# A three-layer graph attention pipeline: score rows of the heads by DMA through DRAM, first values and x one slot earlier

## The chip, the core and the metric

The kernel runs on one core of a Trainium2 chip. The metric is the device time of one execution in microseconds. Its engines are TensorE (PE in the profile), VectorE (DVE), ScalarE (ACT), GpSimd (POOL) and SyncE (SP), which issues all DMAs here. Each works through its own instructions in order; semaphores tie them together. PEld is TensorE's loading of weights.

## The reference, cut to what is computed

There are 16 graphs (batches) of 512 nodes, 256 features and a random adjacency. Layer 1 is attention with four heads of 128 features and an ELU, layer 2 attention with one head of 256, both with the diagonal added to the mask. Then comes a residual with x and a layer norm; layer 3 is one more attention (mask without the diagonal), a leaky ReLU, a residual and a layer norm.

```
def gat_layer(x, mask, W, a_src, a_dst, bias, concat):
    xl = (x @ W).reshape(B, N, H, F)
    asrc = einsum('bnhf,hf->bnh', xl, a_src)
    adst = einsum('bnhf,hf->bnh', xl, a_dst)
    e = leaky_relu(asrc[:, :, None, :] + adst[:, None, :, :], 0.2)
    e = where(mask[..., None], e, -1e9)
    out = einsum('bsdh,bshf->bdhf', softmax(e, axis=1), xl)
...
h = elu(gat_layer(x, mask, W1, ..., concat=True))
h = gat_layer(h, mask, W2, ..., concat=False)
x = layernorm(x + h)
...
Wh = x @ W
e = where(adj > 0, leaky(s_i[:, :, None] + s_j[:, None, :]), -9e15)
x = layernorm(x + leaky(einsum('bij,bjf->bif', softmax(e, axis=1), Wh)))
```

## The kernel before

One attention of one batch is a unit: a head (h0 to h3) of layer 1, the L2 of layer 2, the L3 of layer 3. Units are laid into slots, six to a batch. Slot 0 of batch n has L3 of batch n-3, slots 1 to 4 have the heads of batch n, slot 5 has L2 of batch n-1. Every engine's program is a loop over slots (g, with `n, pos = divmod(g, 6)`), and in it the order of the steps is written out by hand.

A unit takes these steps. `sources_row` (TensorE, line 476 through `spread`) lays the sources' scores as a row over all partitions, with four transposes into the PSUM bank bA, two slots ahead. `tops` (VectorE, line 949, in the slot ahead) adds that row to the turned mask mask_t and takes the largest, four instructions for the four blocks of nodes; `shifted_targets` (lines 962 and 967) makes low and b_t of it, four columns each. `targets_row` (TensorE, line 476 with bB) spreads b_t as a row. In the unit's own slot ScalarE makes leaky (line 741) and exp (756 for heads, 753 for L2, 760 for L3), and VectorE masks with mask_n (`keep_edges`, lines 1000 and 996). In the slot behind, TensorE attends in two halves (`attend`, lines 516, 527, 538). For a head, VectorE then inverts the sums (980), ScalarE normalizes (768) and makes exp (776), VectorE finishes the ELU (974), TensorE turns it (506), and ScalarE and VectorE split it into a high and a low part (782, 986).

Beside the units the slots carry the dense products. First values: `turn_x` (579) turns x, `x_out` (787) and `x_low` (1010) split it, `values_1` (625, 628) multiplies block by block, `values_1_out` (809) copies to val1, which has two buffers. For batch n+1 x is turned in slot 0 of batch n, and the blocks are made in slots 1, 2, 5 and 5. Second values (610) are in slots 2 and 3, third values (598) in slot 4, the turning of x1 (589) in slot 3.

GpSimd has, in order: `scale_3` (419) in slot 0; the scale of the first norm (385, 388), `residual_2` (433, after the first norm x1n of the same slot) and `set_diag` (425) in slot 2; `add_bias_2` (411, after b_t of h3) in slot 3; `norm_2` (385, 388, 394) in slot 4. VectorE's statistics for it (`norm_stats`, 1039 and 1042) stand in slot 5, and `make_mask` (1005) in slot 0. SP issues per batch: four turnings of the mask, the loads of adj and x, the store of an output.

Of the kernel before, what the change touches and what calls it, by code (L numbers as in the profile page):

```python
# [32 lines left out]


def gat_kernel(nc, x, adj, W1, as1, ad1, b1, W2, as2, ad2, b2, W3, a3, out):
# [15 lines left out]
    FIRST, LAST = -SLOTS, SLOTS * B  # L51
# [15 lines left out]

    for i, u in enumerate(units.values()):
        u.u = i
    for i, u in enumerate(u for u in units.values() if u.row):  # L70
        u.r = i

# [11 lines left out]
    with ExitStack() as ctx:  # L84
# [53 lines left out]
        x1_t = sb("x1_t", [P, KD, N])  # L138
        act3 = sb("act3", [P, NB, D])
# [52 lines left out]
        out_stored = sem("out_stored")  # L192

# [59 lines left out]
        for g in range(FIRST, LAST + 1):  # L253
# [19 lines left out]
        for m in (END - 2, END - 1, END):  # L273
            parts = range(len(PARTS) if m == END else 2)
            thirds[m].use = [len(u_uses) + i for i in parts]
            u_uses += [(act3_ready, m * 2 + i + 1) for i in parts]

# [26 lines left out]
        def _(sp):  # L304
# [14 lines left out]

            def turn_mask(n):  # L320
# [26 lines left out]
            load_x(1)  # L347
            for n in range(-1, B):
# [4 lines left out]
                if 2 <= n + 2 < B:  # L353
                    load_x(n + 2)
                if n >= 3:
                    store(n - 3, range(NB))
# [7 lines left out]
        def _(pool):  # L364
# [70 lines left out]
            for g in range(FIRST, LAST):  # L435
# [29 lines left out]
        def _(pe):  # L465
# [13 lines left out]
            def sources_row(u):  # L479
# [6 lines left out]
                if u.u:  # L486
                    pe.wait_ge(top_done, u.u * NB)
# [157 lines left out]
            def first_heads(g):  # L645
# [14 lines left out]
                if g == 5:  # L660
                    sources_row(units[SLOTS + 1])
                if before:
                    attend(before, 1)
                if g == 3:
                    weight_sums()

            pe.wait_ge(consts, 9)
            spread_weights()
            for g in range(FIRST, LAST + 1):
# [9 lines left out]
                if pos == 0 and batch:  # L679
                    turn_x(n + 1)  # L680
                if pos == 2 and batch:
                    values_1(n + 1, 1)
# [4 lines left out]
                if pos == 5 and batch:  # L687
                    values_1(n + 1, 2)
# [6 lines left out]
                if pos == 1 and batch:  # L695
                    if n == -1:
                        pe.wait_ge(w1_lo_ready, 1)
                        pe.wait_ge(bias1_ready, 2 * G)
                    values_1(n + 1, 0)
# [8 lines left out]
                if pos == 5 and batch:  # L708
                    values_1(n + 1, 3)
                if before:  # L710
                    attend(before, 1)
                if later and g < LAST:
                    sources_row(later)
            turn_head(final_head)
# [19 lines left out]
        def _(act):  # L734
# [84 lines left out]
            def first_heads(g):  # L819
# [19 lines left out]
                if g == 5:  # L839
                    act.wait_ge(folded, 2 * KD * H + G + 2 * KH)  # L840
# [4 lines left out]
            for g in range(FIRST, LAST + 1):  # L845
# [6 lines left out]
                if g == -SLOTS:  # L852
                    for k in range(KD):
                        act.wait_ge(w1_in[k], 16 * G)
                        nc.scalar.copy(w1_hi[:, k, :, 0:HC], w1[:, k, :, 0:HC]).then_inc(w1_hi_ready, 1)
# [7 lines left out]
                if pos == 5 and batch:  # L863
                    values_1_out(n + 1, 2)
                if this:
                    leaky(this, (2, 3))
                if pos == 2 and batch:
                    values_1_out(n + 1, 1)
# [6 lines left out]
                if pos == 0 and batch:  # L875
                    x_out(n + 1)
                if pos == 5 and batch:
                    values_1_out(n + 1, 3)
                if pos == 1 and batch:
                    values_1_out(n + 1, 0)  # L880
# [53 lines left out]
        def _(dve):  # L934
# [8 lines left out]
            def tops(u):  # L943

                dve.wait_ge(arow_done, u.u + 1)
                if u.kind == "h" and u.index == 0:
                    dve.wait_ge(mt_loaded, (u.batch + 1) * NB * 16)
                for b in range(NB):
                    nc.vector.tensor_tensor_reduce(junk[:, b] if u.row else att[u.slot % 3][:, b], mask_t[u.batch % 4][:, b],  # L949
                                                   bA[:], 1.0, a_col(u, b) if u.row else LOWEST, ALU.add, ALU.max,  # L950
# [134 lines left out]
            def tops_by_targets(u):  # L1085

                dve.wait_ge(arow_done, u.u + 1)
# [66 lines left out]
            def first_heads(g):  # L1154
# [18 lines left out]
                if g == 5:  # L1173
                    low_weights_2()
# [3 lines left out]
            for g in range(FIRST, LAST + 1):  # L1178
# [8 lines left out]
                if pos == 5 and 0 <= n - 3 < B:  # L1187
                    norm_stats(n - 3, 1, res2, res2_done, 2, stats2, moments2)
# [92 lines left out]
```

## Time and profile before

| | us |
|---|---|
| median of 3 runs | 907.57 (906.18 to 907.77) |
| the profiled execution | 906.74, span 904.8, mean granted clock 0.989 |
| TensorE busy | 861.4 (95%) |
| VectorE busy | 734.1 (81%) |
| ScalarE busy | 690.4 (76%) |
| GpSimd busy | 262.5 (29%) |
| tops of heads and L2 (949), 320 | 219.4, 740 ns each |
| masking of heads (1000), 64 | 150.6, 2353 ns each |
| rows of sources' scores (476, bA), 384 transposes | 58.7 |
| rows of targets (476, bB), 320 transposes | 49.5 |
| x_low (1010), 16 | 19.5, 1217 ns each |
| scaled values (419), 60 | 38.4, 658 ns each |

The span is the time from the first to the last instruction; the execution's own time has some 2 us around it. A line of busy time says how long an engine worked, not whether the end waited for it. For that one reads the chain of waits and, in a stretch of the steady part, what each engine waited for.

### The profile page before, as it was taken

To read this page: it belongs to the slowest core of one execution; us is meant where nothing else is said; L and a number is where in the kernel's file an instruction comes from. 1 tells how busy PE (TensorE), PEld (TensorE's weight loads), DVE (VectorE), ACT (ScalarE), POOL (GpSimd) and SP (SyncE) were. 2 spreads that over 40 slices of the span, in tenths; PEclk is the share of its full clock that TensorE was granted. 3 is DMA by queue.
4 is the path that set the end of the run, shared out by engine and by line. 5 is a ranking of instruction groups with operands and counts; after the bars stand their busy time and mean duration, and the time that the engine had idled before them with its cause. 6 is when DMAs were issued, how large, how long until landed. Compare 5 with 4: busy or idle time off the path is not lost.

```text
span 904.8 us, 17324 instructions
## 1 busy us (share of the span) xinstructions
PE 861.4 (95%) x6220; PEld 813.5 (90%) x6220; DVE 734.1 (81%) x1922; ACT 690.4 (76%) x1288; POOL 262.5 (29%) x244
## 2 busy tenths in 40 slices
PE   6788979999999999999999999999999999999896
PEld 4687879999999999999999999999999999989675
DVE  6776697879788887978888797888879788886866
ACT  2676758789696878879687887968788796878553
POOL 1001011124332332433233243423224342322522
PEclk9898999999999999999999999999999999999999
DMA  7133030301203030120303022030402101000002
GB/s 207 44 95 93 1 93 2 93 1 47 72 24 95 1 117 2 49 70 24 94 1 117 2 48 69 25 94 1 118 1 65 54 24 25 1 24 1 24 1 70
DMA packets 62747, 45.03 MB, mean 50 GB/s; under 512 B 35780, under 2 KB 54340, under 8 KB 62664
## 3 DMA queue, kind: packets, MB, share of 16 engines
q1 hardware_dynamic: 62664, 43.93, 16.7%
q8 instruction: 51, 0.84, 0.4%
q14 instruction: 32, 0.26, 0.1%
HBM read 27.14 MB, written 8.39 MB: 39 GB/s over the span
## 4 chain that ended last, share of the span: by engine, by line
PE 86%; DVE 8%; ACT 3%; issue 2%; DMA 0%; SPq 0%; POOL 0%; POOLq 0%; DVEq 0%; ACTq 0%
PE bUU L516 22%; PE bUU L527 11%; PE bUU L538 11%; PE bG L610 10%; PE bG L628 10%; PE bG L598 5%; PE bA L476 4%; PE bB L476 4%; DVE junk L949 3%; PE bUU L506 3%; PE bG L625 2%; PE bG L589 1%; PE bG L579 1%; ACT att L756 1%; DVE att L1000 1%
## 5 line engine op out<-in xcount | busy, mean ns | idle before, releaser
L516 PE MATMUL bUU<-val,att 128*128 128x129 f32 x2048 | 249.2, 275 | 0.6 <-DVE att L1000 0.6
L516 PEld LDWEIGHTS bUU<-val,att 128*128 128x128 f32 x2048 | 241.4, 192 | 2.6 <-issue 0.8
L949 DVE CUSTOM_DVE_ANT_0 junk<-mask_t,bA,val 128x512 bf16<-128x512 bf16 x320 | 219.4, 740 | 28.3 <-PE bA L476 27.2
L1000 DVE SCALAR_TENSOR_TENSOR att<-mask_n,att 128x2048 f32<-128x2048 bf16 x64 | 150.6, 2353 | 72.7 <-ACT att L756 72.7
L741 ACT ACTIVATE att<-bB,val 128x512 f32<-128x512 f32 x320 | 202.2, 705 | 5.2 <-PE bB L476 5.2
L756 ACT ACTIVATE att<-att 128x2048 f32<-128x2048 f32 x64 | 123.4, 1929 | 0.6
L527 PE MATMUL bUU<-val,att 128*128 128x257 f32 x480 | 109.5, 380 | 3.1 <-DVE res L1030 1.9
L538 PE MATMUL bUU<-val3s,att 128*128 128x256 f32 x480 | 108.3, 379 | 0.2 <-DVE res L1030 0.2
L385 POOL TENSOR_SCALAR var_eps<-moments 128x4 f32<-128x4 f32 x29 | 5.7, 195 | 340.1 <-DVE moments L1042 340.1
L809 ACT COPY val<-bG 128x524 f32<-128x524 f32 x62 | 37.1, 598 | 86.3 <-PE bG L628 84.8
L527 PEld LDWEIGHTS bUU<-val,att 128*128 128x128 f32 x480 | 88.7, 190 | 15.1 <-DVE res L1030 2.3
L538 PEld LDWEIGHTS bUU<-val3s,att 128*128 128x128 f32 x480 | 89.1, 190 | 11.5 <-DVE res L1030 0.6
L394 POOL TENSOR_SCALAR act<-res,moments,rstd 128x256 f32<-128x256 f32 x52 | 91.6, 1769 | 1.5
L768 ACT ACTIVATE x<-bUU,zinv 128x128 f32<-128x128 f32 x256 | 73.1, 370 | 21.7 <-DVE zinv L980 19.9
L610 PE MATMUL bG<-w_hi,y_hi 128*128 128x258 f32 x256 | 75.3, 294 | 0.3 <-DVE y_lo L986 0.3
L610 PE MATMUL bG<-w_hi,y_lo 128*128 128x258 f32 x256 | 72.4, 283 | 0.0
L610 PE MATMUL bG<-w_lo,y_hi 128*128 128x258 f32 x256 | 72.3, 282 | 0.0
L628 PE MATMUL bG<-w_hi,x_hi 128*128 128x262 f32 x248 | 72.0, 290 | 0.0
L628 PE MATMUL bG<-w_lo,x_hi 128*128 128x262 f32 x248 | 71.9, 290 | 0.0
L628 PE MATMUL bG<-w_hi,x_lo 128*128 128x262 f32 x248 | 71.8, 290 | 0.0
L476 PE MATMUL bA<-ident,val 128*128 128x128 f32 x384 | 58.7, 276 | 6.6 <-DVE top L949 5.3
L433 POOL TENSOR_TENSOR res<-act,x1n 128x1024 f32<-128x1024 f32 x13 | 30.9, 2377 | 109.0 <-DVE x1n L1050 109.0
(126 smaller groups left out, 1671.2 us busy)
## 6 DMA issues: line engine op xcount, KB each, us to landing
adj_in<-in_adj_dram SPq DMA_DIRECT2D x16, 1024.0 KB, 5.8
x_in<-in_x_dram SPq DMA_DIRECT2D x16, 512.0 KB, 6.5
out_dram<-act SPq DMA_DIRECT2D x14, 512.0 KB, 2.9
mask_t<-mask_n SPq DMA_TRANSPOSE x64, 2.5
att<-in_L_gnn_W_dram SPq DMA_DIRECT2D x4, 128.0 KB, 3.2
val<-in_L_gnn_W_dram SPq DMA_DIRECT2D x1, 512.0 KB, 7.3
out_dram<-x_in SPq DMA_DIRECT2D x1, 512.0 KB, 2.9
w<-in_L_gnn_W_dram SPq DMA_DIRECT2D x1, 256.0 KB, 6.8
```

The source lines that it names most:

```text
L394: nc.gpsimd.tensor_scalar(act3[:, b], res2[:, b], moments[:, 1, b, 0:1], rstd[:, 1, b:b + 1], ALU.subtract, ALU.mult).then_inc(y_out_done, 1)
L476: ins = nc.tensor.transpose(bank[:, b * P:(b + 1) * P], column(b).to_broadcast([P, P]), ident[:])
L516: ins = nc.tensor.matmul(to[:, (d % 2) * FX:(d % 2 + 1) * FX], p[:, s, d * P:(d + 1) * P], val1[u.batch % 2][:, s, u.index // 2, values], ...
L527: ins = nc.tensor.matmul(to[:, 0:DO + 1], p[:, s, d * P:(d + 1) * P], val2[:, s, 2:DX + 1], start=(s == 0), stop=(s == NB - 1))
L538: ins = nc.tensor.matmul(to[:, d * DO:(d + 1) * DO], p[:, j, (2 * i + d) * P:(2 * i + d + 1) * P], val3s[:, j], start=(j == 0), stop=(j == ...
L610: ins = nc.tensor.matmul(g_bank(b % 2)[:, 0:DX], left[:, k, nodes], right[:, k], start=(k == 0 and i == 0), stop=(k == KH - 1 and i == 2))
L628: ins = nc.tensor.matmul(to, left[:, k, nodes], right[:, k, g], start=False, stop=(k == KD - 1 and i == 2))
L741: nc.scalar.activation(p[:, b], bB[:], ACT.Prelu, bias=a_col(u, b), alpha=SLOPE)\
L756: nc.scalar.activation(flat(p), flat(p), ACT.Exp).then_inc(exp_done, 1)
L768: nc.scalar.activation(x1[u.h % 2][:, d * P:(d + 1) * P], bU[u.use[d // 2] % 4][:, (d % 2) * FX:(d % 2) * FX + F], ACT.Copy, scale=zinv[u. ...
L949: nc.vector.tensor_tensor_reduce(junk[:, b] if u.row else att[u.slot % 3][:, b], mask_t[u.batch % 4][:, b], bA[:], 1.0, a_col(u, b) if u.r ...
L1000: nc.vector.scalar_tensor_tensor(flat(p), mask_n[u.batch % 3][:, 0:NB * N], BIG, flat(p), ALU.add, ALU.min)\
```

## The change

Heads of batch 2 and later (`by_dma`) have no `sources_row` on TensorE. Instead SP stores the four columns of scores of a batch to a DRAM buffer (H x N), and loads each row from there broadcast over the partitions into a new SBUF tensor a_rows. `tops` of these heads reads a_rows instead of bA. For batch n+1 that is issued in iteration n of SP's loop, behind the loads, and each broadcast waits until the tops of the same head of the batch before have read the row.

First values come a slot sooner: for batch n+2 x is turned and block 0 made in slot 5 of batch n, and blocks 1, 2 and 3 in slots 0, 1 and 2 of batch n+1. ScalarE's copies and VectorE's x_low move along. The loads of x for batches 1 to 3 are all issued at the start. The statistics of the second norm move from slot 5 to slot 4 on VectorE. The lead-in of six empty slots is written out as straight code.

```diff
+        self.by_dma = kind == "h" and batch >= 2
...
+    spreading = [u for u in units.values() if not u.by_dma]
+    for i, u in enumerate(spreading):
+        u.a, u.ahead = i, spreading[i - 1] if i else None
...
+        a_rows = sb("a_rows", [P, H, N])
...
+        a_dram = nc.dram_tensor("a_rows_dram", (H, N), F32).ap()
...
+            def store_scores(n):
+
+                sp.wait_ge(val1_ready, (n + 1) * NB)
+                for h in range(H):
+                    if n > 2:
+                        sp.wait_ge(a_spread[h], 16 * (n - 2))
+                    with nc.allow_non_contiguous_dma(reason="columns of scores"):
+                        sp.dma_start(a_dram[h].rearrange("(b p) -> p b", p=P), val1[n % 2][:, :, h // 2, HC + h % 2])\
+                            .then_inc(a_stored, 16)
+
+            def spread_scores(n):
+
+                sp.wait_ge(a_stored, 16 * H * (n - 1))
+                for h in range(H):
+                    if n > 2:
+                        sp.wait_ge(top_done, (units[SLOTS * (n - 1) + 1 + h].u + 1) * NB)
+                    sp.dma_start(a_rows[:, h], a_dram[h].rearrange("(o n) -> o n", o=1).to_broadcast([P, N]))\
+                        .then_inc(a_spread[h], 16)
...
-            load_x(1)
+            for n in range(1, 4):
+                load_x(n)
             for n in range(-1, B):
                 if n + 1 < B:
                     turn_mask(n + 1)
                 if 1 <= n + 2 < B:
                     load_adj(n + 2)
-                if 2 <= n + 2 < B:
+                if 4 <= n + 2 < B:
                     load_x(n + 2)
+                if 2 <= n + 1 < B:
+                    store_scores(n + 1)
+                    spread_scores(n + 1)
...
-                if u.u:
-                    pe.wait_ge(top_done, u.u * NB)
+                if u.ahead:
+                    pe.wait_ge(top_done, (u.ahead.u + 1) * NB)
...
                     sources_row(units[SLOTS + 1])
+                    turn_x(2)
                 if before:
                     attend(before, 1)
                 if g == 3:
                     weight_sums()
+                if g == 5:
+                    values_1(2, 0)
...
+            turn_x(0)
+            pe.wait_ge(w1_lo_ready, 1)
+            pe.wait_ge(bias1_ready, 2 * G)
+            for b in range(NB):
+                values_1(0, b)
+            sources_row(units[1])
...
-                if pos == 0 and batch:
-                    turn_x(n + 1)
                 if pos == 2 and batch:
-                    values_1(n + 1, 1)
+                    values_1(n + 1, 3)
                 if pos == 3 and second:
                     values_2(n - 1, (2, 3))
                 if pos == 4 and third:
                     values_3(n - 2, (0, 1))
-                if pos == 5 and batch:
-                    values_1(n + 1, 2)
+                if pos == 5 and n + 2 < B:
+                    turn_x(n + 2)
...
-                if pos == 1 and batch:
-                    if n == -1:
-                        pe.wait_ge(w1_lo_ready, 1)
-                        pe.wait_ge(bias1_ready, 2 * G)
-                    values_1(n + 1, 0)
+                if pos in (0, 1) and batch:
+                    values_1(n + 1, pos + 1)
...
-                if pos == 5 and batch:
-                    values_1(n + 1, 3)
                 if before:
                     attend(before, 1)
-                if later and g < LAST:
+                if later and not later.by_dma and g < LAST:
                     sources_row(later)
+                if pos == 5 and n + 2 < B:
+                    values_1(n + 2, 0)
             turn_head(final_head)
...
-                if pos == 5 and batch:
-                    values_1_out(n + 1, 2)
+                if pos == 5 and n + 2 < B:
+                    x_out(n + 2)
+                if pos == 0 and batch:
+                    values_1_out(n + 1, 0)
                 if this:
                     leaky(this, (2, 3))
                 if pos == 2 and batch:
-                    values_1_out(n + 1, 1)
+                    values_1_out(n + 1, 3)
                 if pos == 3 and second:
                     values_2_out(n - 1, (2, 3))
                 if pos == 4 and third:
...
-                if pos == 0 and batch:
-                    x_out(n + 1)
-                if pos == 5 and batch:
-                    values_1_out(n + 1, 3)
-                if pos == 1 and batch:
-                    values_1_out(n + 1, 0)
+                if pos in (0, 1) and batch:
+                    values_1_out(n + 1, pos + 1)
...
-                dve.wait_ge(arow_done, u.u + 1)
+                if u.by_dma:
+                    dve.wait_ge(a_spread[u.index], 16 * (u.batch - 1))
+                else:
+                    dve.wait_ge(arow_done, u.a + 1)
...
-                                                   bA[:], 1.0, a_col(u, b) if u.row else LOWEST, ALU.add, ALU.max,
+                                                   a_rows[:, u.index] if u.by_dma else bA[:], 1.0, a_col(u, b) if u.row else LOWEST, ALU.add, ALU.max,
...
-                if pos == 5 and 0 <= n - 3 < B:
-                    norm_stats(n - 3, 1, res2, res2_done, 2, stats2, moments2)
...
-                if n == -1 and pos == 0:
-                    x_low(0)
-                    make_mask(0)
-                    fold_2()
-                    fold_3()
-                elif pos == 0 and n + 1 < B:
+                if pos == 0 and n + 1 < B:
                     make_mask(n + 1)
-                    x_low(n + 1)
+                if pos == 5 and n + 2 < B:
+                    x_low(n + 2)
                 if g == LAST - 1:
                     invert(final_head)
+                if pos == 4 and 0 <= n - 3 < B:
+                    norm_stats(n - 3, 1, res2, res2_done, 2, stats2, moments2)
                 if this and this.row:
                     keep_edges(this)
```

## Rows read from the trace of the kernel before

**Rows 1.** The page: share of the span of the chain that ended last, by engine.
```profile
PE 86%; DVE 8%; ACT 3%; issue 2%; DMA 0%; SPq 0%; POOL 0%; POOLq 0%; DVEq 0%; ACTq 0%
```

**Rows 2.** Busy time of each engine in one batch: stretch, its length, engines, clock, DMA.
```profile
446.40:498.95 52.55, 52.55 (x390) 50.19 (x390) 44.15 (x114) 42.73 (x81) 18.07 (x15) 1.00 0.17 51
```

**Rows 3.** Chain of waits in this batch: start, duration in us, what.
```profile
451.06 0.44 PE bA L476 x4
...
469.79 1.79 PE bUU L516 x16
...
472.02 0.12 PE bG L625
472.14 0.73 PE bG L628 x6
...
476.82 3.47 PE bUU L527 x16
```

**Rows 4.** Timeline of TensorE: start, duration, engine, line, output and inputs, idle before.
```profile
451.26 0.37 PE L610 MATMUL bG<-w_hi,y_hi 128*128 128x258 f32 x1
...
456.02 0.60 PE L476 MATMUL bB<-ident,b_t 128*128 128x128 f32 x4
...
463.52 0.60 PE L476 MATMUL bB<-ident,b_t 128*128 128x128 f32 x4
...
467.85 0.37 PE L625 MATMUL bG<-bias,ones_r 128*128 128x262 f32 x1
...
480.57 0.60 PE L476 MATMUL bB<-ident,b_t 128*128 128x128 f32 x4
...
811.13 0.65 PE L476 MATMUL bB<-ident,b_t 128*128 128x128 f32 x4 [1.66 <-DVE b_t L967]
```

**Rows 5.** Timeline of VectorE, of the same batch, and its first tops.
```profile
24.84 0.75 DVE L949 CUSTOM_DVE_ANT_0 junk<-mask_t,bA,val 128x512 bf16<-128x512 bf16 x1 [3.12 <-PE bA L476]
...
454.53 0.16 DVE L967 SCALAR_TENSOR_TENSOR b_t<-top,low 128x4 f32<-128x4 f32 x1
456.72 2.56 DVE L1000 SCALAR_TENSOR_TENSOR att<-mask_n,att 128x2048 f32<-128x2048 bf16 x1 [2.03 <-ACT att L756]
...
459.81 0.23 DVE L980 RECIPROCAL zinv<-bUU 128x2 f32<-128x2 f32 x2
...
463.06 0.16 DVE L967 SCALAR_TENSOR_TENSOR b_t<-top,low 128x4 f32<-128x4 f32 x1
464.82 2.29 DVE L1000 SCALAR_TENSOR_TENSOR att<-mask_n,att 128x2048 f32<-128x2048 bf16 x1 [1.60 <-ACT att L756]
...
468.38 1.38 DVE L1039 BATCH_NORM_STATS2 stats<-res 128x6 f32<-128x256 f32 x4
...
479.39 0.16 DVE L967 SCALAR_TENSOR_TENSOR b_t<-top,low 128x4 f32<-128x4 f32 x1
```

**Rows 6.** Timeline of ScalarE, same batch.
```profile
457.10 1.07 ACT L792 COPY x_t<-bG 128x512 f32<-128x512 f32 x2 [0.47 <-PE bG L589]
...
468.50 1.14 ACT L768 ACTIVATE x<-bUU,zinv 128x128 f32<-128x128 f32 x4 [0.44 <-DVE zinv L980]
```

**Rows 7.** The page, DMA issues: what, count, KB each, us to landing.
```profile
x_in<-in_x_dram SPq DMA_DIRECT2D x16, 512.0 KB, 6.5
```

**Rows 8.** Timeline of VectorE near the end, beside the next group.
```profile
843.43 2.17 DVE L962 SCALAR_TENSOR_TENSOR low<-top,val 128x4 f32<-128x4 f32 x1
```

**Rows 9.** Timeline of GpSimd in the same stretch.
```profile
843.24 2.35 POOL L411 TENSOR_TENSOR x_in<-x_in,bias 128x1024 f32<-128x1024 f32 x1
```

**Rows 10.** GpSimd's second norm, line 394: ns least/median/most, first and last start.
```profile
L394 POOL TENSOR_SCALAR act<-res,moments,rstd x52: 1218/1261/3323, 208.8 to 842.1; 128x256 f32<-128x256 f32 x52
```

**Rows 11.** Timeline of GpSimd in slot 3 of the batch at 446 us.
```profile
450.53 2.38 POOL L433 TENSOR_TENSOR res<-act,x1n 128x1024 f32<-128x1024 f32 x1 [8.62 <-DVE x1n L1050]
452.87 1.17 POOL L425 TENSOR_TENSOR mask_n<-mask_n,ident_big 128x512 bf16<-128x512 bf16 x1
454.77 2.36 POOL L411 TENSOR_TENSOR x_in<-x_in,bias 128x1024 f32<-128x1024 f32 x1 [0.74 <-DVE b_t L967]
```

More of the change, by code:

```diff
@@ L49, in gat_kernel @@
     assert F == P and N == 512 and H == 4 and KH == H and DO == D and W3.shape[1] == DO and KD == 2
-    FIRST, LAST = -SLOTS, SLOTS * B
+    LAST = SLOTS * B
     END = B - 1
@@ L192, in gat_kernel @@
         out_stored = sem("out_stored")
+        a_stored = sem("a_stored")
+        a_spread = [sem(f"a_spread{i}") for i in range(H)]
         xt_turned = sem("xt_turned")
@@ L252, in gat_kernel @@
         u_uses = []
-        for g in range(FIRST, LAST + 1):
+        for g in range(LAST + 1):
             u, older = units.get(g - 1), head_at(g - 3)
@@ L433, in residual_2 @@
                 nc.gpsimd.tensor_tensor(flat(res2), flat(act3), flat(x1n[m % 2]), ALU.add).then_inc(res2_done, 2)
-            for g in range(FIRST, LAST):
+            set_diag(0)
+            for g in range(LAST):
                 n, pos = divmod(g, SLOTS)
@@ L665, in first_heads @@
                     weight_sums()
+                if g == 5:
+                    values_1(2, 0)
             pe.wait_ge(consts, 9)
             spread_weights()
-            for g in range(FIRST, LAST + 1):
+            turn_x(0)
[4 more added lines that the diff above has]
+            sources_row(units[1])
+            for g in range(LAST + 1):
                 n, pos = divmod(g, SLOTS)
@@ L839, in first_heads @@
                 if g == 5:
+                    x_out(2)
                     act.wait_ge(folded, 2 * KD * H + G + 2 * KH)
@@ L844, in _ @@
             nc.scalar.activation(warm[:], neg_one[:], ACT.Exp).then_inc(warmed, 1)
-            for g in range(FIRST, LAST + 1):
+            for k in range(KD):
+                act.wait_ge(w1_in[k], 16 * G)
+                nc.scalar.copy(w1_hi[:, k, :, 0:HC], w1[:, k, :, 0:HC]).then_inc(w1_hi_ready, 1)
+            x_out(0)
+            for b in range(NB):
+                values_1_out(0, b)
+            for g in range(LAST + 1):
                 n, pos = divmod(g, SLOTS)
@@ L851, in _ @@
                 third, second, batch = 0 <= n - 2 < B, 0 <= n - 1 < B, 0 <= n + 1 < B
[L852 to L855, printed above, removed]
                 third_layer = units.get(g - 2) if pos == 2 else None
@@ L1085, in tops_by_targets @@
             def tops_by_targets(u):
-                dve.wait_ge(arow_done, u.u + 1)
+                dve.wait_ge(arow_done, u.a + 1)
                 for b in range(NB):
@@ L1173, in first_heads @@
                 if g == 5:
+                    x_low(2)
                     low_weights_2()
@@ L1177, in _ @@
             fold_1()
-            for g in range(FIRST, LAST + 1):
+            x_low(0)
+            make_mask(0)
+            fold_2()
+            fold_3()
+            for g in range(LAST + 1):
                 n, pos = divmod(g, SLOTS)
```

## The prediction

> **What bounds the kernel now.** I read the page first. The chain that ended last is 86% TensorE [rows 1], so the question is whether TensorE ever waits. The stretch table of one batch in the middle says no: in 52.55 us TensorE is busy for all of them, at full clock, while VectorE has 44.15 and ScalarE 42.73 us of work [rows 2]. Batches 3 to 14 all have this period. The chain of waits through such a batch [rows 3] is then a list of TensorE's work and a price list: a row laid out by four transposes 0.44 us, turning x (eight transposes) so 0.87, one block of first values (0.12 + 0.73) twice = 1.7, half of a head's attention 1.78, half of L2's 3.47. From the start of one piece to that of the next the prices are the same in the timeline, whose starts lie 0.17 earlier [rows 4].
>
> A kernel bound by one engine gains what is taken from that engine, until the next limit. So the second reading is the slack of what feeds TensorE. The timelines of one batch give it. Each slot has a loop: VectorE finds the tops and the shifted targets b_t, TensorE spreads b_t into bB, ScalarE makes leaky and exp, VectorE masks, TensorE attends a slot later. b_t of the next batch's head 0 ends at 479.39 + 0.16 = 479.55 [rows 5], and TensorE takes it up at 480.57 [rows 4]: slack 1.0 us. b_t of head 3 ends at 454.69 and is taken at 456.02: slack 1.3. b_t of L2 ends at 463.22 and is taken at 463.52: slack 0.3. These slacks are all smaller than or like what is removed. In the last batch, where TensorE has less to do, it does wait for b_t, 1.66 us (the row at 811.13 [rows 4]); there the delay began with a row in bA, which the change removes for heads.
>
> **The change part by part, with the clock of the batch at 446 us.**
>
> *Removed from TensorE:* four rows of sources' scores for each of batches 2 to 15: 4 x 0.44 = 1.75 us a batch [rows 3], 24.6 us over 14 batches if nothing else binds: 882.
>
> *Moved on TensorE:* the turning of x from slot 0 to the slot before it (5), first values from slots 1, 2, 5, 5 to 5, 0, 1, 2. From the start of slot 5 (467.85 [rows 4]) to the spreading of head 0's b_t, TensorE had 12.72 us (480.57 - 467.85). Now it has turning x 0.87, head 3's attention 3.56, a turned head 0.44, one block 1.7, L2's first half 3.47 and a turned head 0.44: 10.5. It arrives 2.2 us sooner against 1.0 us of slack. VectorE and ScalarE don't get sooner there: ScalarE has two copies (1.07, as those of x1 at 457.10 [rows 6]) after its normalization at 468.50, in place of a short wait and one copy of values (0.6 + 0.19), so its exp comes 0.3 later; VectorE loses the statistics of slot 5 (from 468.38, 1.6 with their gathering [rows 5]), gets the low part of x (1.2), and waits for that exp. b_t of head 0 then ends at about 479.85, TensorE stands 1.4 us, and of 1.75 only 0.35 is left.
>
> *Moved on VectorE:* the second norm's statistics go from slot 5 to slot 4, into a wait of 1.60 us for the exp of head 3, before the masking at 464.82 [rows 5]. Free, as long as that wait is there.
>
> *Added DMAs.* Per batch four stores of 512 pieces of 4 bytes and four broadcasts of 256 KB, all on SP behind the loads. Values are ready in slot 2; the first tops that read the rows come about 32 us later (from 445 to 477). The nearest row is a load of x, 512 pieces of 1 KB, 6.5 us to landing [rows 7]. Two such landings one after another, the four of a kind overlapping, are 13 us, all eight in series 52; no gain is possible. I take 13, since the pieces carry 4 bytes and not 1 KB: hidden. Behind them on SP wait the store of an output and the next mask's turning, neither due before slot 0. If that cover is gone, every microsecond beyond 32 is one in each batch. At the start two more x loads (1 MB) go ahead of the first mask's turning; VectorE's first tops wait 3.12 us for TensorE there, at 24.84 [rows 5], so 0 to 2 us, and I take 0.
>
> *What the tops read.* Before, tops read the mask from SBUF and the row from PSUM (bA). Now both inputs are in SBUF. The trace shows what this does beside GpSimd. A four-column operation of two SBUF inputs (low, from top), which like that for b_t takes 0.16 us [rows 5], took 2.17 us at 843.43 and ended with the GpSimd addition of 843.24 to 845.59 that ran beside it [rows 8, 9]. The masking at 456.72 took 2.56 and not 2.29 as that at 464.82, beside the end of such an addition [rows 5, 11]. The other way, GpSimd's scaling has a minimum of 1.22 and a maximum of 3.32 us, where a masking lies across it [rows 10]. And the tops of head 3, with one operand in PSUM, now run through GpSimd's residual and diagonal (450.53 to 454.04 [rows 11]) at the 0.74 each that they take everywhere, undisturbed. The Trainium skill says the same in "SBUF — State Buffer", section "SBUF: two separate sides": the second port is an exclusive lock, held for a whole instruction, between GpSimd and a VectorE operation with two SBUF inputs. The trace agrees for the operations named above. That the rule takes in the new tops too, no row shows; without it the sum would be that of rival 1, with it the one that follows.
>
> *The sum with the lock.* Slot 3 starts at 451.26; what hangs on the values of slot 2 comes 0.4 later against it, since head 3's row is gone from between. So GpSimd's residual runs 450.95 to 453.33 and lets go 0.14 before its end (2.56 - 2.29 = 0.27 of the 0.41 by which it overlapped). Tops of head 3 ask at 451.7 and start at 453.2: four at 0.67 (0.74 less overlap), 455.9. The diagonal's addition (1.17) stands waiting and gets the port at the first gap, which is there at the latest where the shifted targets wait for the tops; these too are two-input operations. b_t ends at 453.2 + 2.7 + 1.1 + 0.35 = 457.35, and TensorE wanted it at 456.02: 1.35, with restart 1.45 us.
> Then masking of head 2 to 459.7. GpSimd's bias addition (2.36) is let off by b_t too and takes the port at 459.7, before the next two-input operation, whose exp ScalarE has ready only at 460.2 since TensorE turned x1 later. elu ends at 462.55, the inverse of head 1 at 462.7 instead of 460.0. From it tops and targets of L2 take 3.26 (459.96 to 463.22 [rows 5]): 466.0, where TensorE stands at 463.52 + 1.45 = 464.97: 1.0 more, 2.5 together. ScalarE's exp of head 3, 2.9 later than before, comes at 467.6; masking of it to 469.95, the low part, elu and the inverse of head 2 at 471.4. From the normalization of head 2 to b_t of head 0 the time before was 479.55 - 468.50 = 11.05 [rows 5, 6], now 0.3 more: 471.45 + 11.35 = 482.8. TensorE, from 467.85 + 2.5, gets there at 480.85, and 0.15 for the low part of x: 1.8 more. Stalls 4.45, removed 1.75: **+2.7 us a batch**. It holds for batches 3 to 14, which have all three GpSimd steps: 12 x 2.7 = 32.4. Batches 1, 2 and 15 come out at about nothing (batch 15 gets back its 1.66 [rows 4] and pays slot 3). The profiled execution takes 906.74, its span 904.8; 906.74 + 32.4 = 939.1, and the median of the runs is 0.8 above it: **940**. Its own range: +1.6 a batch if stalls overlap better to +4 if the tops of head 1 also hold up GpSimd's scaled values in slot 1, which TensorE then needs in 2 us: 925 to 956.
>
> **Rivals.**
> 1. *No lock for these tops.* Then 0.35 to 0.5 a batch over 13 batches and 1.66 + 1.75 in the last: 8 to 10 less, 898 (894 to 903). For it: no row shows this operation with both inputs in SBUF. Against: every two-input operation that met a long GpSimd addition was held up. This is the side of faster. It decides from where tops of head 3 start before GpSimd's residual ends.
> 2. *The lock, but the targets get past the diagonal's addition.* b_t of head 3 ends at 453.2 + 2.7 + 0.35 = 456.25, stall 0.25; the bias addition then falls beside one-input tops, TensorE doesn't stop for L2, head 0's b_t is 0.6 later: stall 1.8. 0.3 + 0.5 for slot 1 a batch: +4 to +14, 914. For it: GpSimd's scaling of 3.32 us lay across a masking in two instructions back to back, and did not get in between them [rows 10]. Against: the targets must wait for the tops' result, and that is a gap.
> 3. *The rows come late.* The 128 pieces per DMA engine would have to take over 150 ns each ((32 - 13) / 128); +1 us a batch for each 8 ns beyond. 950. No row speaks for it. The page "DMA: Bandwidth & Descriptors" (Trainium skill, Specifications) says that below 512 B the engine reads, modifies and writes; it gives no time for 4 bytes.
>
> **How the numbers follow.** Lock with the diagonal ahead 0.46, rival 2 0.21, rival 1 0.27, rival 3 0.06. Likeliest: 940. Range 897 to 952: it takes in rival 1 to about its middle, all of rival 2, and the main case but for its top. No change means within 0.2% (about what a measurement of this kernel can tell), 905.8 to 909.4: the low edge of rival 2, 0.04. Faster 0.28 (rival 1, and 0.01 for rival 2), slower 0.68. The sign hangs on a row that the trace of before can't have: tops with both inputs in SBUF.
>
> **What would show it.** The TensorE rows for L476 should fall by 224 transposes. Right: tops of head 3 (slot 3) with a first instance of 1.5 to 2.2 us and not 0.74; TensorE waiting for b_t three times a batch, 1.4, 1.0 and 1.8; batch period 55.3. Rival 1: tops all at 0.74, one wait of 1.4 a batch, period 52.1. Rival 2: the first at 2 us, targets at 0.17, period near 53. Rival 3: VectorE idle before L949, released by a DMA. Wrong altogether if b_t's wait is gone and the period is near 50.8: then the order of ScalarE and VectorE in slot 5 was read wrongly.

## The result, and the profile after

The changed kernel takes 931.76 us (931.02 to 932.84, 4 runs) against 907.32 (906.18 to 907.77, 4 runs): ratio 1.0272, interval 1.0254 to 1.029. It is slower by 24.4 us, as forecast in sign; 940 was forecast, 32.4 us more than before. The profiled span is 930.9 us.

The page after, its chain by engine and the groups that moved (busy us, mean ns of one, then idle time before them):

```profile
PE 50%; DVE 27%; ACT 13%; issue 9%; another core or an unknown queue 0%; DMA 0%; POOL 0%; DVEq 0%; SPq 0%; POOLq 0%; ACTq 0%
...
L992 DVE CUSTOM_DVE_ANT_0 junk<-mask_t,a_rows,val 128x512 bf16<-128x512 bf16 x224 | 189.7, 901 | 0.0
L562 PE MATMUL bUU<-val,att 128*128 128x257 f32 x480 | 113.2, 384 | 16.0 <-ACT x L807 13.1
...
L419 POOL TENSOR_SCALAR var_eps<-moments 128x4 f32<-128x4 f32 x29 | 32.3, 1115 | 235.8 <-DVE moments L1085 235.8
...
L511 PE MATMUL bB<-ident,b_t 128*128 128x128 f32 x320 | 51.4, 284 | 34.1 <-DVE b_t L1010 31.8
```

Where the chain was 86% TensorE [rows 1] it is now half, and VectorE and ScalarE have 40%. TensorE waits for b_t 31.8 us in all (11.6 before) and for ScalarE's normalization before L2 13.1. The tops that read a_rows take 901 ns in the mean, where all tops took 740. One batch, 526.04 to 580.56 us, against [rows 2]:

```profile
526.04:580.56 54.52, 51.91 (x373) 48.50 (x373) 48.34 (x114) 41.97 (x80) 21.15 (x16) 1.00 0.25 69
```

The numbers are the stretch, its length, the busy time of TensorE, of its weight loading, of VectorE, ScalarE and GpSimd, the granted clock, the DMA share and GB/s. The period is 54.52 us and not 52.55: +1.97. VectorE and GpSimd have the same instructions in a batch and are busy 4.2 and 3.1 us longer: that is waiting inside instructions, which the profile counts as busy. The clock is the same.

Not the whole loss lies in these periods. The table follows the profiled executions: how many us later than in the kernel before TensorE spreads head 1's b_t in batch 3 and in batch 15, and how many later the last instruction ends. The runs below the first row are the experiments of the next section.

| | at batch 3 | at batch 15 | end of the span |
|---|---|---|---|
| changed kernel | 5.2 | 28.3 | 26.1 |
| row in PSUM | 5.2 | 1.4 | -1.6 |
| shift alone | 7.2 | 16.8 | 14.8 |
| head 3's row by TensorE | 5.3 | 8.7 | 6.5 |
| GpSimd sooner | 5.0 | 3.3 | 4.2 |
| row in PSUM, wait filled | 2.6 | -9.1 | -12.1 |
| GpSimd sooner, wait filled | 2.7 | -8.5 | -7.5 |

So the changed kernel loses 5.2 us before batch 3 is under way, 23.1 in the twelve batches 3 to 14 (12 x 1.97 is 23.6), and gets 2.2 back at the end. The first part is there with the row in PSUM too. Most of it, 4.4, stands already at head 1's b_t of batch 1 (76.32 us against 71.94); a block of values for batch 2 is now made just ahead of it. No run takes that block away by itself, so its cause is not shown.

Slot 3 of this batch. First VectorE, then GpSimd, to be held against [rows 5] and [rows 11]:

```profile
520.36 2.29 DVE L992 CUSTOM_DVE_ANT_0 junk<-mask_t,a_rows,val 128x512 bf16<-128x512 bf16 x1
522.58 1.63 DVE L992 CUSTOM_DVE_ANT_0 junk<-mask_t,a_rows,val 128x512 bf16<-128x512 bf16 x1
524.14 0.74 DVE L992 CUSTOM_DVE_ANT_0 junk<-mask_t,a_rows,val 128x512 bf16<-128x512 bf16 x1
524.82 0.74 DVE L992 CUSTOM_DVE_ANT_0 junk<-mask_t,a_rows,val 128x512 bf16<-128x512 bf16 x1
...
525.80 0.16 DVE L1010 SCALAR_TENSOR_TENSOR b_t<-top,low 128x4 f32<-128x4 f32 x1
525.88 2.29 DVE L1043 SCALAR_TENSOR_TENSOR att<-mask_n,att 128x2048 f32<-128x2048 bf16 x1
528.87 2.06 DVE L1017 SCALAR_TENSOR_TENSOR y<-e,x 128x512 f32<-128x512 f32 x1 [0.70 <-ACT e L815]
```

```profile
519.71 2.39 POOL L467 TENSOR_TENSOR res<-act,x1n 128x1024 f32<-128x1024 f32 x1 [8.79 <-DVE x1n L1093]
522.06 1.60 POOL L459 TENSOR_TENSOR mask_n<-mask_n,ident_big 128x512 bf16<-128x512 bf16 x1
526.04 4.34 POOL L445 TENSOR_TENSOR x_in<-x_in,bias 128x1024 f32<-128x1024 f32 x1 [2.38 <-DVE b_t L1010]
```

The first of head 3's tops lies across the end of GpSimd's residual (2.29 us for 0.74), the second across the diagonal's addition (1.63), which itself takes 1.60 for 1.17. Then the bias addition lies under the masking (4.34 for 2.36) and comes out on the other side to hold the ELU (2.06 for 0.68). TensorE in the same batch, to be held against [rows 4]:

```profile
522.97 1.95 PE L551 MATMUL bUU<-val,att 128*128 128x129 f32 x16
526.02 0.65 PE L511 MATMUL bB<-ident,b_t 128*128 128x128 f32 x4 [1.10 <-DVE b_t L1010]
...
534.33 0.65 PE L511 MATMUL bB<-ident,b_t 128*128 128x128 f32 x4 [0.60 <-DVE b_t L1010]
...
538.78 1.04 PE L614 MATMUL bG<-ident,x_in 128*128 128x128 f32 x8
...
545.67 1.90 PE L562 MATMUL bUU<-val,att 128*128 128x257 f32 x8
548.43 2.00 PE L562 MATMUL bUU<-val,att 128*128 128x257 f32 x8 [0.87 <-ACT x L807]
...
550.85 0.65 PE L511 MATMUL bB<-ident,b_t 128*128 128x128 f32 x4
```

Three waits a batch, in the slots of the forecast: head 3's b_t, L2's b_t, and one in slot 0. The last does not stand before head 0's b_t but 2.4 us ahead, before the second quarter of L2's attention, which needs the PSUM bank that ScalarE's normalization of head 3 empties.

The rows themselves come early. SP's waits over the run (us in total, times, longest):

```profile
SPq L347 <- DMA a_rows_dram<-val: 148.1, 14, 11.3
```

After it has issued four stores of 512 pieces of 4 bytes (some 2 us), SP waits 10.6 us in the mean until they have landed; a broadcast of 256 KB takes 3.9 (median). The broadcasts issued from 525.9 on are there by 532, their first reader comes at 547.6. No tops wait for a row.

### The profile page after: what moved, and what is told of

Its sections match the earlier page's. It is cut to its first block, busy times and chain, and to the rows that moved or that the text cites. A ratio compares the mean times of both kernels' runs of the same rounds, so it can differ in the third digit from the quotient of the medians.

```text
span 930.9 us, 16958 instructions
## 1 busy us (share of the span) xinstructions
PE 852.8 (92%) x5996; PEld 791.0 (85%) x5996; DVE 785.3 (84%) x1922; ACT 689.8 (74%) x1288; POOL 294.4 (32%) x244
## 3 DMA queue, kind: packets, MB, share of 16 engines
q1 hardware_dynamic: 100296, 58.73, 23.1%
## 4 chain that ended last, share of the span: by engine, by line
PE 50%; DVE 27%; ACT 13%; issue 9%; another core or an unknown queue 0%; DMA 0%; POOL 0%; DVEq 0%; SPq 0%; POOLq 0%; ACTq 0%
PE bUU L573 10%; DVE junk L992 10%; PE bUU L562 8%; PE bG L645 8%; PE bG L663 8%; PE bUU L551 7%; DVE y L1017 4%; PE bB L511 3%; ACT x L807 3%; DVE y_lo L1029 2%; ACT att L780 2%; DVE stats L1082 2%; DVE att L1039 2%; ACT att L795 2%; ACT att L792 2%
## 5 line engine op out<-in xcount | busy, mean ns | idle before, releaser
L1043 DVE SCALAR_TENSOR_TENSOR att<-mask_n,att 128x2048 f32<-128x2048 bf16 x64 | 153.6, 2399 | 50.9 <-ACT att L795 50.9
L992 DVE CUSTOM_DVE_ANT_0 junk<-mask_t,a_rows,val 128x512 bf16<-128x512 bf16 x224 | 189.7, 901 | 0.0
L562 PE MATMUL bUU<-val,att 128*128 128x257 f32 x480 | 113.2, 384 | 16.0 <-ACT x L807 13.1
L419 POOL TENSOR_SCALAR var_eps<-moments 128x4 f32<-128x4 f32 x29 | 32.3, 1115 | 235.8 <-DVE moments L1085 235.8
L453 POOL TENSOR_SCALAR val3s<-val,z3inv 128x256 f32<-128x256 f32 x60 | 49.1, 832 | 137.8 <-DVE z3inv L1060 134.7
L511 PE MATMUL bB<-ident,b_t 128*128 128x128 f32 x320 | 51.4, 284 | 34.1 <-DVE b_t L1010 31.8
L511 PEld LDWEIGHTS bB<-ident,b_t 128*128 128x128 f32 x320 | 35.3, 139 | 44.6 <-DVE b_t L1010 42.1
```

The lines of the kernel that those rows point to most:

```text
L453: nc.gpsimd.tensor_scalar(val3s_of(m, b), val3[m % 2][:, b, 2:DX], z3inv[:, b:b + 1], 1.0, ALU.mult, ALU.mult)\
L511: ins = nc.tensor.transpose(bank[:, b * P:(b + 1) * P], column(b).to_broadcast([P, P]), ident[:])
L562: ins = nc.tensor.matmul(to[:, 0:DO + 1], p[:, s, d * P:(d + 1) * P], val2[:, s, 2:DX + 1], start=(s == 0), stop=(s == NB - 1))
L1043: nc.vector.scalar_tensor_tensor(flat(p), mask_n[u.batch % 3][:, 0:NB * N], BIG, flat(p), ALU.add, ALU.min)\
```

## The experiments

Each edit is to the changed kernel and is shown cut to its main lines. Ratios are to the kernel before, run on the same chip. Periods are the distance between two mask makings of neighbouring batches.

**The operand alone.**

```diff
-                if u.ahead:
-                    pe.wait_ge(top_done, (u.ahead.u + 1) * NB)
+                if u.u:
+                    pe.wait_ge(top_done, u.u * NB)
...
+                    dve.wait_ge(arow_done, max(v.a for v in spreading if v.u < u.u) + 1)
...
-                                                   a_rows[:, u.index] if u.by_dma else bA[:], 1.0, a_col(u, b) if u.row else LOWEST, ALU.add, ALU.max,
+                                                   bA[:], 1.0, a_col(u, b) if u.row else LOWEST, ALU.add, ALU.max,
```

> The changed kernel with one operand swapped: tops of the heads by DMA read the row that lies in the PSUM bank bA instead of a_rows in SBUF. All DMAs, all waits on them and the moved work stay. The row in bA is another unit's, so the maxima that shift the targets are not the right ones; nothing else is left out. Theory (port of two-SBUF-input tops shared with GpSimd costs the time): tops all at 0.74, batch period 52.1, 898 us (894 to 904). Rival A (the moved x and first values cost it) and rival B (the rows' DMAs cost it): 925 to 932, no change from the changed kernel.

Measured: 904.7 us, ratio 0.9968 (0.9955 to 0.9981), period 52.30. All tops in a long stretch of it:

```profile
L993 DVE CUSTOM_DVE_ANT_0 junk<-mask_t,bA,val x208: 719/740/748, 245.6 to 779.9; 128x512 bf16<-128x512 bf16 x104
```

Least 719, most 748 ns: no instance is held up. One operand's place is worth 27 us. Neither the moved work nor the DMAs can be the cause of these 27 us, as both are still there. But it stops at 905, not 898 (its range was 894 to 904). What TensorE still waits for, between 250 and 750 us:

```profile
PE bUU L562 <- ACT x L807: 8.6, 10, 0.9
PE bB L511 <- DVE b_t L1011: 0.7, 1, 0.7
```

**The shift alone.**

```diff
-        self.by_dma = kind == "h" and batch >= 2
+        self.by_dma = False
...
-                if 2 <= n + 1 < B:
-                    store_scores(n + 1)
-                    spread_scores(n + 1)
```

> The changed kernel without the rows by DMA: all rows by TensorE as before, only x, first values and the statistics a slot sooner. Theory (TensorE now reaches head 0's b_t before VectorE has it): a wait of about 1.0 us a batch, period 53.5, 920 us (914 to 926). Rival A' (the shift is free, the whole loss is in the tops' operand): 907. Rival A (the shift is the whole loss, and rows by TensorE cost 1.75 more): 950.

Measured: 920.96 us, ratio 1.0145 (1.0129 to 1.016), period 53.5, as the theory has it. The shift by itself costs 13.4 us against 907.55 on the same chip: TensorE gets to slot 0 before VectorE and ScalarE. Its wait there is not for head 0's b_t, as the expectation has it, but for ScalarE's normalization before L2's second quarter (0.5 us a batch). And the sum fits in part by luck: 7.2 of the 13.4 us come before batch 3, which the expectation left out (the table above). So the loss has two parts, 27 us by the operand and 13 by the shift; the rows saved on TensorE (920.96 to 904.7 with the row in PSUM, 16 us) pay for the second and little more.

**Head 3's row by TensorE.**

```diff
-        self.by_dma = kind == "h" and batch >= 2
+        self.by_dma = kind == "h" and batch >= 2 and index < 3
```

> The changed kernel with head 3's row laid out by TensorE again, so that its tops read PSUM; heads 0 to 2 stay by DMA. Theory: only head 3's tops meet GpSimd's residual and diagonal, so both waits for b_t in slots 3 and 4 vanish, 0.44 of TensorE work a batch comes back, what is left is the wait before head 0's b_t: period 52.5, 905 us (900 to 911). Rival (the collisions are no cause): 932 + 14 x 0.44 = 938.

Measured: 912.28 us, ratio 1.0052 (1.0037 to 1.0067). The sign and most of the size are there: giving 6 us of work back to TensorE makes it 19.5 us faster. It is 7 us above the 905 expected and outside the range. The longest of the tops that read a_rows is now 961 ns:

```profile
L992 DVE CUSTOM_DVE_ANT_0 junk<-mask_t,a_rows,val x120: 728/746/961, 272.6 to 768.1; 128x512 bf16<-128x512 bf16 x120
```

Most periods are 52.63, against 52.5 expected, but three are 53.84, 53.88 and 54.14, which adds 4.0 us. In each of them TensorE waits once for L2's b_t (0.80 to 1.11 us). In the first, ScalarE's copy of second values ahead of head 2's exp starts 1.5 us later than in the batch after it; what holds it there is not shown. The 5.3 us before batch 3 stayed out of the expectation too.

**Head 3's row alone by DMA.**

```diff
-        self.by_dma = kind == "h" and batch >= 2
+        self.by_dma = kind == "h" and batch >= 2 and index == 3
```

> Only head 3's row by DMA, heads 0 to 2 by TensorE: the part of the change that collides, alone. Theory: changed kernel less head 3 by TensorE is 19.5 us, and 6 us of TensorE work saved lie in it, so the collisions cost 25.6; added to the shift alone (921.0), less 6: 940 us (934 to 945), slower than all four by DMA. Rival (the loss comes with the number of rows by DMA, here a quarter): 920 to 924.

Measured: 942.97 us, ratio 1.0402 (1.0383 to 1.0421), within the range. One head by DMA is slower than four. TensorE's waits between 240 and 780 us:

```profile
PE bB L511 <- DVE b_t L1010: 16.9, 20, 1.1
PE bUU L562 <- ACT x L807: 7.0, 10, 0.7
```

Two waits for b_t a batch, as in the changed kernel. The loss does not grow with the number of rows; it is where head 3's tops stand.

**The diagonal out of the way.**

```diff
+                if pos == 2 and 0 <= n + 1 < B:
+                    set_diag(n + 1)
                 if pos == 2 and 0 <= n - 2 < B:
                     norm_scale(n - 2, 0, moments1, var1, rstd1)
...
-                if pos == 2 and 0 <= n + 1 < B:
-                    set_diag(n + 1)
```

> The changed kernel with GpSimd's diagonal addition before the first norm's scale in slot 2, not behind the residual: one of the three GpSimd steps is out of the way of head 3's tops. Theory: b_t of head 3 1.1 us sooner, its wait nearly gone, the bias addition may still meet the ELU: period 53.3, 917 us (908 to 922). Rival (only the residual matters): 929 to 932.

Measured: 924.94 us, ratio 1.0182 (1.0165 to 1.0199), period 53.83. Faster by 6.8, between the two expectations and outside both ranges: the addition costs 0.7 us a batch and not 1.1. The longest of the tops is still 2289 ns, as in the changed kernel, for the residual is still in front of them.

**The statistics put back to slot 5,** ahead of the tops, as in the kernel before.

```diff
+                if pos == 5 and 0 <= n - 3 < B:
+                    norm_stats(n - 3, 1, res2, res2_done, 2, stats2, moments2)
                 if g == LAST:
...
-                if pos == 4 and 0 <= n - 3 < B:
-                    norm_stats(n - 3, 1, res2, res2_done, 2, stats2, moments2)
```

> The changed kernel with the second norm's statistics back in slot 5, one part of the change undone. Theory: in slot 4 VectorE has no wait left (the collisions took it), so the move there costs 1.7 us which slot 5 gives back; undone, masking of head 3 is 1.7 sooner, but GpSimd's scaling reaches tops of head 0, where the port is held up: 932 to 945. Rival (the move of the statistics cost part of the loss): 920 to 928.

Measured: 945.74 us, ratio 1.0422 (1.0406 to 1.0438). The move of the statistics saves 14 us. The time is 0.7 us above what was expected (932 to 945), and the loss is there, but not for the reason given there. TensorE's waits, 240 to 780 us:

```profile
PE bB L511 <- DVE b_t L1010: 17.0, 20, 1.1
PE bG L660 <- DVE x_lo L1053: 13.4, 10, 1.3
PE bUU L562 <- ACT x L807: 5.0, 10, 0.5
```

There is a new wait of 1.3 us a batch for the low part of x, which stands behind the statistics in VectorE's slot 5 and which TensorE needs for the first block of values there. Head 0's tops lose little there: in one batch the first takes 0.90 us (at 385.91) beside GpSimd's scaling, the other three 0.74.

**Filling the wait in slot 0.** TensorE makes block 1 of the next values while it would wait for the bank: `attend_2_first` does one quarter of L2's attention, and the block goes between two of them. In ScalarE's program (the last two pieces of the diff) block 0 is copied before head 3 is normalized.

```diff
-                if before:
+                between = pos == 0 and batch and before is not None
+                if between:
+                    attend_2_first(before, 0)
+                    values_1(n + 1, 1)
+                    attend_2_first(before, 1)
+                elif before:
                     attend(before, 0)
...
-                if pos in (0, 1) and batch:
+                if pos in (0, 1) and batch and not between:
                     values_1(n + 1, pos + 1)
...
+                if pos == 0 and batch:
+                    values_1_out(n + 1, 0)
                 if older:
                     normalize(older)
...
-                if pos == 0 and batch:
-                    values_1_out(n + 1, 0)
```

> The changed kernel with the same filling of L2's wait, all four heads by DMA. Theory: the collisions in slot 3 stay, the wait in slot 0 goes: 1.0 us a batch less, 920 us (916 to 925). Rival (slot 0's wait is a consequence of the delay that begins in slot 3, and VectorE sets the period): 929 to 932.

Measured: 920.24 us, ratio 1.0138 (1.0124 to 1.0152), 11.5 less than the changed kernel. The wait for the bank is gone and two waits for b_t a batch stay (17.3 us in 20, between 240 and 780 us). So slot 0's wait can be had by itself, with the collisions in slot 3 still there. With the row in PSUM:

> Tops read the row in the PSUM bank bA (another unit's, so the maxima are not the right ones), with the filling of L2's wait. It is what the change could bring with both costs gone: period 51.3, 892 us (888 to 897). Rival (VectorE and ScalarE set the period next): 901 to 904.

Measured: 894.21 us, ratio 0.9855 (0.9841 to 0.9868), most periods 51.5: 10.5 less than without the filling. And with head 3's row by TensorE:

> Heads 0 to 2 by DMA, head 3 by TensorE, and the wait that is left is filled: in slot 0 the block 1 of first values goes between the first and the second quarter of L2's attention, where TensorE waited 0.9 us for the bank that ScalarE's normalization of head 3 frees, and ScalarE copies block 0 ahead of that normalization. Theory: about 1.0 us a batch less than head 3 by TensorE alone (912.3), 13 x 1.0: 900 us (896 to 904), under the kernel before (907.5). Rival (the wait only moves to head 0's b_t): 910 to 912.

Measured: 900.54 us, ratio 0.9931 (0.9918 to 0.9943), under the kernel before.

**GpSimd's two steps of slot 2 sooner, all heads by DMA.** The diagonal first as above; the residual in halves, each adding its own batch's x1n as before, but without the wait for the x1n that VectorE makes in the same slot, which had put it late in the slot.

```diff
-                pool.wait_ge(act3_ready, 2 * (m + 1))
...
-                nc.gpsimd.tensor_tensor(flat(res2), flat(act3), flat(x1n[m % 2]), ALU.add).then_inc(res2_done, 2)
+                for half in range(2):
+                    two = slice(2 * half, 2 * half + 2)
+                    pool.wait_ge(act3_ready, 2 * m + half + 1)
+                    nc.gpsimd.tensor_tensor(res2[:, two].rearrange("p b n -> p (b n)"), act3[:, two].rearrange("p b n -> p (b n)"),
+                                            x1n[m % 2][:, two].rearrange("p b n -> p (b n)"), ALU.add).then_inc(res2_done, 1)
...
-                if pos == 2 and 0 <= n - 2 < B:
-                    pool.wait_ge(x1n_done, (n - 1) * NB)
```

> The same without the filling: the changed kernel with GpSimd's two steps of slot 2 sooner. Theory: the collisions gone, slot 0's wait left, as with the row in PSUM (904.7): 906 us (903 to 910). Rival: 918 to 932.

Measured: 911.76 us, ratio 1.0054 (1.0039 to 1.0069): 20 us less than the changed kernel, 6 more than expected. The period is 52.44, against 52.30 with the row in PSUM, so the steady batches do what was expected; of the 5.8 us between the two profiled executions 5.2 come after head 1's b_t of batch 14. With the filling:

> All four heads by DMA and the filling of L2's wait, and GpSimd's steps of slot 2 out of the way: the diagonal addition first in the slot, the residual in two halves of 512 columns, each as soon as its half of the third layer is there and not behind x1n. Theory: no long GpSimd addition is left before head 3's tops, so the time is nearly that of the row in PSUM with the same filling (894.2): 896 us (893 to 900), under head 3 by TensorE with the filling (900.5). Rival (the halves now hold up masking of head 1 and x1n, and the tops again): 908 to 920.

Measured: 899.11 us, ratio 0.9912 (0.9898 to 0.9927), the fastest version that computes everything, 8 us under the kernel before. Its VectorE in slots 2 and 3, and GpSimd beside it:

```profile
343.28 2.34 DVE L1108 TENSOR_SCALAR x1n<-res,moments,rstd 128x256 f32<-128x256 f32 x4
345.69 0.73 DVE L1007 CUSTOM_DVE_ANT_0 junk<-mask_t,a_rows,val 128x512 bf16<-128x512 bf16 x1
...
388.46 1.77 DVE L1007 CUSTOM_DVE_ANT_0 junk<-mask_t,a_rows,val 128x512 bf16<-128x512 bf16 x1
```

```profile
341.53 2.96 POOL L469 TENSOR_TENSOR res<-act,x1n 128x512 f32<-128x512 f32 x1 [3.44 <-ACT act L870]
...
388.23 1.45 POOL L469 TENSOR_TENSOR res<-act,x1n 128x512 f32<-128x512 f32 x1
```

The first of head 3's tops takes 0.73 us now. The collisions went elsewhere: one half of the residual holds up x1n (2.34 for 1.38) and another one of head 2's tops (1.77). The rival's mechanism is there, but in the steady batches not its price: the period is 51.60, against 51.5 with the row in PSUM, and up to head 1's b_t of batch 14 this kernel is not behind that one (744.17 us against 744.49). That 894 is not reached comes from the last two batches. There the halves meet head 2's tops of batch 15, and TensorE, which has less to do, has to wait for them. GpSimd's two halves, two of these tops and TensorE:

```profile
800.23 3.21 POOL L469 TENSOR_TENSOR res<-act,x1n 128x512 f32<-128x512 f32 x2
...
800.57 1.75 DVE L1007 CUSTOM_DVE_ANT_0 junk<-mask_t,a_rows,val 128x512 bf16<-128x512 bf16 x1
802.25 1.74 DVE L1007 CUSTOM_DVE_ANT_0 junk<-mask_t,a_rows,val 128x512 bf16<-128x512 bf16 x1
...
804.45 1.11 PE L512 MATMUL bB<-ident,b_t 128*128 128x128 f32 x4 [3.88 <-DVE b_t L1025]
```

From 740 us on TensorE waits 6.1 us for b_t here, and 3.0 with the row in PSUM. Without the filling it is the same: 6.4 and 3.0.

## Why the prediction was right, point by point

- **TensorE bounds the kernel before; 24.6 us to be had if nothing else binds.** The price of a row held: with TensorE free of both costs (row in PSUM, wait filled) the kernel took 894.2, so some 13 of the 24.6 can be had. Batches 3 to 14 give 11.7 of it and the end 3.0, and 2.6 are lost before batch 3. The steady period is 51.5 and not the 50.8 of 52.55 less 1.75; what fills this 0.7 is shown only in part, TensorE waits 0.34 us a batch in what the profile names.
- **The shift meets VectorE and ScalarE in slot 0.** Right in size: a wait of 1.4 with the rows saved was forecast, a period of 52.1, and 52.30 was measured; the shift alone gave a period of 53.5 as expected. Wrong in place: the wait stands before L2's second quarter, for a bank. The step by which TensorE gets to head 0's b_t at 480.85 did not look at who frees the banks that L2 writes. Both hang on the same chain in VectorE, so the time came out nearly the same: in the batch shown VectorE ends head 0's b_t at 550.80 (550.63 + 0.17), and TensorE, without the wait for the bank, would have stood there from 538.78 + 10.5 = 549.3, an estimate.
- **Statistics in slot 4 free, as long as the wait is there.** Undone, the kernel is 14 us slower, but for another reason: the statistics in slot 5 delay x's low part. Whether they are free in slot 4, where the wait had gone, is not tested by itself.
- **DMAs hidden.** Right: some 15 us to spare in the batch shown. The trip was put at 13 us; it took 2 of issue, 10.6 and 3.9, so 16 to 17.
- **Two inputs in SBUF take the port that GpSimd uses.** Right for GpSimd's long additions, and it decides the sign: 27 us with one operand's place. This was the step that no row of before could show; the rows on other operations carried over. The first of head 3's tops takes 2.29 us, just over the 1.5 to 2.2 given as the sign of it. So the rule of the Trainium skill ("SBUF — State Buffer", "SBUF: two separate sides") holds for these tops and GpSimd's additions too. Its "whole instruction" does not hold for GpSimd's scalings, which let a two-input operation in before their end (541.96 us, last section).
- **The sum.** The mechanism was right, the size too large: 32.4 us were forecast, 24.4 measured. It is as near as that partly by luck, for two errors offset each other. For batches 3 to 14 32.4 were forecast and 23.1 measured; for all else about nothing, and before batch 3 it was 5.2, at the end -2.2. (These are the profiled executions, 26.1 us apart.) Forecast were 4.45 us of stalls a batch, less 1.75 saved. Measured, in the batch shown: from the attention ahead of head 3's targets to these targets TensorE takes 3.05 us (522.97 to 526.02) where it took 1.78 (454.24 in the row below to 456.02 in [rows 4]), so 1.27 and not 1.45. From there to L2's targets 8.31 where it took 7.50, so 0.81 and not 1.0. From the start of slot 5 to head 0's targets 12.07 for 10.5 of work, so 1.57 and not 1.95: the last term was missed the most. The remaining slots cost next to nothing. 3.65 less 1.75 is 1.90 of the +1.97. One reason is that the diagonal's addition did not wait for all four tops but got in after the first, and its start overlapped with it: it cost 0.7 us a batch and not 1.1.

```profile
454.24 1.95 PE L516 MATMUL bUU<-val,att 128*128 128x129 f32 x16
```

- **Rival 1** (no lock) was put at 898. The same order of work with the row in PSUM takes 904.7. The difference is mostly the 5.2 us before batch 3, which the sum of this rival left out too; the steady batches gave 0.25 and not 0.35 to 0.5, and what follows head 1's b_t of batch 15 gave 3.0, near the 3.4 put down for the last batch. The case itself is out, by the tops of 2.29 us. **Rival 2** (targets get past the diagonal) is out: the diagonal went ahead even earlier. Its upper +14 is also more than its terms give, 0.3 + 0.5 over 13 batches, 10.4. **Rival 3** (late rows) is out, with 15 us to spare.
- The measured time lies within the range (897 to 952) and within its case's own range (925 to 956). The range is wide, as it takes in two rivals; it is the tops of 2.29 us and the three waits that speak for the mechanism, not the number.

What stays open: what costs the 5.2 us before batch 3, and what delays ScalarE in the three long periods of head 3's row by TensorE.

## What to carry to other kernels

Moving an operand from PSUM to SBUF can give VectorE's instruction a second SBUF input, and then, as far as these runs show, it and every long GpSimd addition exclude each other: look in the timeline for what GpSimd runs beside it, and at which of them the next engine waits. An instruction that waits for the port shows as busy and long, not as idle; compare least and most duration of a group, not its mean. And where a bound engine is relieved by 1.75 us a batch, look first for 1.75 us of slack in what feeds it; here the same saving was worth 3 us with the operand in PSUM (904.7 against 907.55), and 13 once one block of other work was put into the wait that it opened (894.2). And follow a loss along the run: a steady period times the number of batches leaves out the lead-in and the end, 5.2 and -2.2 us here.

## What the runs showed of the hardware that was not expected

- GpSimd gets the port in the gap between one of the tops and the next, which have the read of the accumulator between them (the diagonal's addition after the first of four), but did not get in between the two instructions of L2's masking, which stand back to back ([rows 10]: 3.32 us for 1.22).
- VectorE's x1n, a scaling with one tensor input, was held up too: 2.34 us for four, where they take 1.38, beside half a residual of GpSimd (2.96 us).
- GpSimd's smallest operation can wait as long as the large ones: var_eps, four columns, took 2.25 us behind a masking, and 1115 ns in the mean over the changed kernel's run (195 before).

```profile
535.96 2.25 POOL L419 TENSOR_SCALAR var_eps<-moments 128x4 f32<-128x4 f32 x1 [5.58 <-DVE moments L1085]
```

- GpSimd's scaling of 128x256 (1.22 us) keeps a two-input operation for a part of its time only. In the changed kernel, beside the scaling that started at 541.84, low at 541.96 took 0.45 us for its 0.17, and b_t at 542.44, 0.6 us into the same scaling, took its usual 0.16.
- 2048 pieces of 4 bytes (8 KB) to DRAM need 10.6 us in the mean after the last issue, longer than 512 KB of x in 512 pieces (6.7 us).
